# A spectral-convolution tower on one Trainium2 core: activations and mix weights moved in four and two DMAs instead of one

## What is computed

```python
x = coords @ fc0_w + fc0_b
for sw, cw, cb in (...):                # four layers
    x1 = _spectral_conv(x, sw)          # rfft2, 20 x 20 modes mixed over channels, irfft2
    x2 = einsum('bchw,oc->bohw', x, cw) + cb
    x = gelu(x1 + x2)
h = gelu(x @ fc1_w + fc1_b) @ fc2_w + fc2_b
h = h + attention(layernorm(h))
h = h + experts(layernorm(h))
```

## Time and profile before

| What | us |
|---|---|
| Median of 3 runs | 1694.77 |
| Lowest, highest | 1679.24, 1694.86 |
| The profiled execution | 1695.4 |
| Span of its instructions | 1693.6 |

### The profile page before, as it was taken

How to read it: one execution, slowest core, us unless ns; L and a number is a source line. 1 busy time by engine, 2 the same in 40 slices (tenths; PEclk the granted TensorE clock), 3 DMA queues, 4 the chain that set the end, 5 groups by cost and what they waited for, 6 DMA issues and landing times. The chain is left out here.

```text
span 1693.6 us, 68354 instructions
## 1 busy us (share of the span) xinstructions
PE 1434.8 (85%) x32216; PEld 731.4 (43%) x32216; DVE 1181.6 (70%) x1433; ACT 534.0 (32%) x673; POOL 92.3 (5%) x45
## 2 busy tenths in 40 slices
PE   8888888887888888888888888777777999989997
PEld 3444444454444444544444445444442113872332
DVE  3499999977889888689888887343340002987877
ACT  2422222222222222222222222322325998440222
POOL 1000000000000000000000000000000000006551
PEclk9999999999999999999999999888988999998998
DMA  5333242365565656565656564777777774018430
GB/s 209 104 127 141 114 152 107 123 229 202 201 247 210 231 217 230 182 220 217 235 204 241 209 220 158 264 256 257 281 281 279 276 267 145 21 41 192 112 92 13
DMA packets 60056, 317.82 MB, mean 188 GB/s; under 512 B 16704, under 2 KB 18688, under 8 KB 25984
## 3 DMA queue, kind: packets, MB, share of 16 engines
q1 hardware_dynamic: 36512, 177.95, 32.5%
q10 hardware_dynamic: 23264, 135.49, 19.5%
HBM read 176.05 MB, written 137.36 MB: 185 GB/s over the span
## 5 line engine op out<-in xcount | busy, mean ns | idle before, releaser
L836 ACT ACTIVATE act_c<-slots,conv_b 128x1024 f32<-128x1024 f32 x256 | 283.2, 1114 | 861.5 <-PE slots L552 861.5
L725 DVE STREAM_TRANSPOSE inv_out<-slots 128x1024 f32<-128x1024 f32 x256 | 304.8, 1229 | 209.9 <-PE slots L514 209.9
L552 PEld LDWEIGHTS slots<-inv_w,inv_out 64*64 64x64 f32 x16384 | 287.4, 139 | 295.0 <-issue 284.4
L552 PE MATMUL slots<-inv_w,inv_out 64*64 64x64 f32 x16384 | 325.0, 228 | 91.0 <-issue 85.4
L701 DVE STREAM_TRANSPOSE turned_h<-slots 128x1024 f32<-128x1024 f32 x200 | 235.7, 1219 | 52.0 <-PE slots L447 52.0
L447 PE MATMUL slots<-turned_w,fwd_w 32*64 32x512 f32 x3200 | 217.8, 624 | 34.7 <-DVE inv_out L725 27.3
L514 PE MATMUL slots<-turned_k,inv_h 64*64 64x320 f32 x2048 | 183.7, 469 | 73.1 <-DVE turned_h L701 45.9
L690 DVE STREAM_TRANSPOSE turned_w<-act_c 128x1024 f32<-128x1024 f32 x192 | 224.7, 1212 | 0.0
L536 PE MATMUL slots<-act_c,conv_w 32*32 32x512 f32 x3072 | 127.5, 658 | 18.1 <-issue 12.7
L514 PEld LDWEIGHTS slots<-turned_k,inv_h 64*64 64x64 f32 x2048 | 77.1, 140 | 150.5 <-DVE turned_h L701 89.2
L459 PE MATMUL slots<-turned_h,fwd_h 64*64 64x320 f32 x1600 | 134.4, 444 | 1.8 <-DVE turned_h L701 1.3
(11 more groups left out here) (166 smaller groups left out, 1120.2 us busy)
## 6 DMA issues: line engine op xcount, KB each, us to landing
act_scratch<-act_c ACTq DMA_DIRECT2D x128, 1024.0 KB, 6.2
act_c<-act_scratch SPq DMA_DIRECT2D x128, 1024.0 KB, 5.8
mode_w<-in_sw_dram SPq DMA_DIRECT2D x20, 640.0 KB, 4.2
at_turned<-level_scratch SPq DMA_DIRECT2D x24, 256.0 KB, 4.1
at_ret_t<-level_scratch SPq DMA_DIRECT2D x20, 256.0 KB, 4.3
xin<-in_x_dram SPq DMA_DIRECT2D x4, 1024.0 KB, 8.2
turned_w<-in_x_turned_dram SPq DMA_DIRECT2D x3, 1024.0 KB, 4.8
at_straight<-level_scratch SPq DMA_DIRECT2D x10, 256.0 KB, 4.4
```

Of the source, the lines that this page charges most:

```text
L552: mm = nc.tensor.matmul(banks[half * 64:(half + 1) * 64, 2 * two + odd, at:at + 64], inv_out[rows, t % 2, i, two, s, 2 * half:2 * half + 2 ...
L725: nc.vector.transpose(dst, src).then_inc(inv_turned, 1)
L836: nc.scalar.activation(act_c[:, t % RING, :, at, :].rearrange("p i q m -> p q i m"), banks[:, at, :].rearrange("p q (i m) -> p q i m", i=2 ...
```

## The change

Every load and store of a pair's activations becomes four DMAs, each over all 128 partitions and a quarter of the columns: 256 KB with rows of 2 KB where before 1 MB went with rows of 8 KB. Every load of mix weights becomes two DMAs of 320 KB with rows of 2.5 KB, where before 640 KB went with rows of 5 KB. All parts of one load add to the semaphore that the whole added to before, and the waits count 64 instead of 16 per use of a slot of act_c, and 32 instead of 16 for mode_w. No wait is added or moved; the loads of xin are as before.

```diff
+ACT_PARTS = 4
+MODE_PARTS = 2
...
         def after_load(l, t):
-            return 16 * ((l - 1) * (PAIRS // RING) + t // RING + 1)
+            return 16 * ACT_PARTS * ((l - 1) * (PAIRS // RING) + t // RING + 1)
 
         def after_store(l, t):
-            return 16 * (l * (PAIRS // RING) + t // RING + 1)
+            return 16 * ACT_PARTS * (l * (PAIRS // RING) + t // RING + 1)
+
+
+        def part_of(n, parts, size):
+
+            return slice(n * (size // parts), (n + 1) * (size // parts))
...
-                sp.dma_start(flat(mode_w[:, n % RING_W]), sw[l, pair]).then_inc(mode_w_in[n % RING_W], 16)
+                for k in range(MODE_PARTS):
+                    cols = part_of(k, MODE_PARTS, 2 * MIXES * 2 * CH)
+                    sp.dma_start(flat(mode_w[:, n % RING_W])[:, cols], sw[l, pair][:, cols]).then_inc(
+                        mode_w_in[n % RING_W], 16)
...
-                sp.dma_start(flat(act_c[:, t % RING]), act_dram[t]).then_inc(act_in[t % RING], 16)
+                for k in range(ACT_PARTS):
+                    cols = part_of(k, ACT_PARTS, 2 * 4 * 256)
+                    sp.dma_start(flat(act_c[:, t % RING])[:, cols], act_dram[t][:, cols]).then_inc(
+                        act_in[t % RING], 16)
...
-                        pe.wait_ge(mode_w_in[n % RING_W], 16 * (n // RING_W + 1))
+                        pe.wait_ge(mode_w_in[n % RING_W], 16 * MODE_PARTS * (n // RING_W + 1))
...
-                    act.dma_start(act_dram[t], flat(act_c[:, t % RING])).then_inc(act_stored[t % RING], 16)
+                    for k in range(ACT_PARTS):
+                        cols = part_of(k, ACT_PARTS, 2 * 4 * 256)
+                        act.dma_start(act_dram[t][:, cols], flat(act_c[:, t % RING])[:, cols]).then_inc(
+                            act_stored[t % RING], 16)
```

## The result

| | Median us | Range | Runs |
|---|---|---|---|
| Before | 1694.03 | 1679.24 to 1694.86 | 4 |
| After | 1719.01 | 1717.71 to 1733.39 | 4 |

The ratio is 1.0188, with a 95% interval from 1.011 to 1.0265: slower, by 25 us between the medians and by 32 us by the ratio, which is formed from the means. The forecast was 1631 us and faster. The profiled execution of after is its longest run (1733.4 us, span 1731.6), so its stages add up to 38 us more than before, where the medians differ by 25. In the sections that follow, the few runs that fell into a slower state are left out of the ratios, but not of the medians.

A forecast was written before the change was run, and what follows sets the result against it. TensorE was taken to wait for its instruction fetch behind activation packets. Gains of 27 us (layers 1, 2), 2 (layer 0) and 40 (layer 3), less 5 at starts, make 64: 1695.4 us to 1631, range 1600 to 1690.

The forecast's parts named there:

- What bounds the kernel: TensorE stops for its own instruction fetch, queued behind activation packets: 63.9 us in layer 3, 18.9 and 23.8 in layers 1, 2.
- I take 80%: Layers 0 to 3: quarter-size DMAs let the instruction fetch in sooner, removing 80% of TensorE's stops, bounds 0 and 100%.
- I take 87 ns: Activation DMAs: a 2 KB packet holds a DMA engine 87 ns, at most some 200 ns for loads.
- the line: Packet times: straight line through 20 ns (256 B stores) and 316 ns (8 KB stores), giving 87 ns at 2 KB.
- the transfers are late next: Layer 3: transfers, 6.15 us a pair at 0.93 full, limit it to 212 us, so 40 us gained instead of 51.
- Rival (c): Layer 3: small packets make DMA engines the bound, from about 140 ns per 2 KB load packet; 1725 us, chance 0.09.
- Rival (a): Fetch wait: bytes queued on an engine hold up the fetch, not row count; half the gains, 1666 us, chance 0.13.
- 0.81 of a stop reaches the end: Layers 0 to 2: 0.81 of stop time lengthens the layer; 27 us gained in layers 1 and 2, 2 in layer 0.
- Issues, starts, mix weights: Four issues per load or store hidden; 5 us lost at layer and head starts; split mix weights nothing, within 4 us.
- Rival (d): Layers 0 to 3: without stops TensorE's clock stays at 2.4 GHz, transfers reach 0.97 full; 1609 us, chance 0.08.
- (b): Fetch wait lies ahead of the DMA engines, so the split has no effect; 1695 us, perhaps 1700, chance 0.10.

The follow-up runs named there:

- e_tiny1: Kernel before the change, with each activation load and store moving only 64 of a partition's 2048 numbers: 1590.01 us, ratio 0.9418.
- e_block4: Changed kernel with each quarter a contiguous 256 KB block in DRAM, mix weights whole: 1666.23 us, ratio 0.9874 to the kernel before.
- e_strided4: Changed kernel with mix weights as one DMA again, rows still 8 KB apart: 1723.17 us, ratio 1.0164 to the kernel before.
- e_pitch8q: Changed kernel with mix weights whole and scratch rows 8.25 KB apart: 1670.20 us, ratio 0.9897 to the kernel before.
- e_tiny4: Changed kernel with each of the four DMAs moving 64 numbers of a partition instead of 512, mix weights whole: 1592.95 us.
- e_pitch10: Changed kernel with mix weights whole and scratch rows 10 KB apart: 1671.13 us, ratio 0.986 to the kernel before.

## Why the prediction was wrong

**What bounds the kernel: right.** TensorE's "issue" is its instruction fetch, held up by activation traffic. e_tiny1 shows that the traffic causes most of it: the kernel takes 104 us less, and of the 85.2 us of stops in layers 1 and 3 only 24.1 are left. That it is the fetch rests on the earlier trace rows and on the same picture in e_block4: 256 instructions from stop to stop, and the q8 packet just before TensorE goes on.

**"I take 80%" of the stops: this step failed.** With contiguous blocks 9% of the stops went, not 80%; in the changed kernel they grew. The step from "a whole load went ahead of the fetch" to "the fetch waits for one DMA of each queue" had no row behind it: the earlier trace rows show what passed before the fetch, not what it waited for. In three delays of e_block4 1.9, 2.8 and 4.3 quarters of loads went ahead of the fetch, where the step needs one. Of the 63.9 us, 24.1 remain even with almost no traffic. The Trainium skill (DMA: Bandwidth & Descriptors, section "Queues, rings and completion order") lets an engine change queues only at the end of a packet of descriptors. That stops shrink at four and eight parts agrees with it; that a quarter-size DMA gives a quarter of the wait the runs do not bear out.

**"I take 87 ns" for a 2 KB packet: right for stores, wrong for loads.** Stores in layer 1 took 43.6 us per MB (0.279 x 16 x 327.8 / 33.56), 89 ns. Loads took 116 ns, for two reasons. The upper end of the line, 316 ns, is of stores alone; whole loads took 394 ns in layer 1, and a line through 20 and 394 ns gives 104, which is what rows close together or off the 8 KB distance took (50.8 to 51.9 us per MB, 104 to 106 ns). The rest is that the changed kernel has its rows exactly 8 KB apart, and I never asked where a quarter's rows lie in DRAM. All rows of my trace were of contiguous blocks. That one property is worth 45 to 53 us (e_strided4 against e_pitch8q) and decides the sign: without it the ratio is 0.986 to 0.9897, 17 to 24 us faster instead of 25 to 32 slower.

**How slower loads turned the sign: by a term that the sum does not have.** It prices a packet only in "the transfers are late next". The transfers of a pair took 6.3 us of all engines in layer 3 (0.76 x 266.5 / 32) against 6.15 in the forecast; at 0.93 full that is 218 us instead of 212 for the layer, and the forecast would have been 1637 us. They were not late: the DMA share stayed at 0.76. Instead the stops grew, in layer 3 by 18.9 us where the layer grew by 14.3, in layer 1 by 15.8 where it grew by 13.9. From e_pitch8q to e_strided4, where only the distance differs, they go from 78.0 to 107.3 us in the two layers. That slower packets keep the queues filled longer and so hold up more fetches is my account of it; no run shows the step itself. Rival (c) had the right sign by the wrong road: the packets stayed under its 140 ns and the transfers never bound layer 3. Rival (a) had what holds the fetch up, what is queued, but not its price.

**0.81 of a stop reaches the end: the number held, its reading did not.** Layer 1 is 13.4 us longer than layer 0, but by the earlier trace rows 10.0 of them are TensorE's busy time and only 3.4 are idle. e_tiny1 wins 17.0 us for 21.3 us of stops, again mostly as busy time: that the factor came out right is luck. Beside it stands a small slip, 5.67 and 0.5 are 6.2 and not 6.15, which would make the 212 us of layer 3 213.

**Issues, starts, mix weights: right in the main.** 3 us for four issues by e_tiny4, which holds what was put on the starts too; the mixes take 14.4, 12.3 and 13.5 us where they took 14.4, 12.5 and 13.2; the mix weights in two parts cost nothing; the head is unchanged at 133.6 us.

**Rival (d)'s clock is real.** e_tiny1 frees it in full; but in layer 3 of e_block4 and e_pitch10 too the granted clock is 0.92 instead of 0.86, and TensorE is busy 7.5 and 9.8 us less. That is more than the stops by themselves gave in e_block4 (3.3 us). The forecast left it out of its sum.

The rule that spoke against the change, at least 1 MiB per DMA (Trainium skill, DMA: Bandwidth & Descriptors, section "Rules for kernel authors"), is one on bandwidth. In engine time the runs agree with it, 48.1 us per MB whole and 51.9 in contiguous quarters. The kernel was faster with 256 KB and 512 KB all the same where the rows were placed well.

The forecast gave 0 to 100% as bounds for the share of the stops that goes, and did not carry the 0% into its range of 1600 to 1690: (b), which is that end, was left out at 1695 to 1700. Even it would not have reached 1719, since nothing in the working let the stops grow.

## What to carry to other kernels

When a DMA is cut by columns, look at the distance of its rows in DRAM before anything else: at 8 KB it cost some 50 us of 1670 here, and 256 bytes of padding, or a scratch laid out by parts, gave it back. Where a long unrolled program stops without a waiting semaphore, count instructions between the stops and look at the instruction queue; run it once with hardly any traffic to see how much of the stops can be had. A transfer's packets seen ahead of a fetch do not say that cutting the transfer lets the fetch in: the next parts may go ahead of it as well. Count TensorE's busy time and its granted clock beside its stops, since much of what traffic cost here was there.

## What the runs showed that was not expected

Rows 16 KB apart cost less (53.7 us per MB, 1687 us) than rows 8 KB apart (57.8, 1723 us). A DMA onto 32 partitions with 8 KB rows needs 51.9 us per MB stored, where one onto 128 needs 38.9, and the kernel with four such DMAs per load and store is 3.8% slower.
